# Differential attention on one core: the steps of TensorE written as two interleaved streams, one per row group

## What is computed

```python
Q = einsum('bse,hec->bhsc', X, Wq) + bq      # c = 2 * 64
K = einsum('bse,hec->bhsc', X, Wk) + bk
V = einsum('bse,hed->bhsd', X, Wv) + bv
A1 = einsum('bhqd,bhkd->bhqk', Q1, K1) * s   # first 64 of c
A2 = einsum('bhqd,bhkd->bhqk', Q2, K2) * s   # last 64 of c
P = softmax(A1) - lam * softmax(A2)
O = einsum('bhqk,bhkd->bhqd', P, V)
Y = concat_heads(O) @ Wo + bo                # then layer norm, gamma, beta
```

## Time and profile before

| | us |
|---|---|
| median of 3 runs | 1207.48 (1206.95 to 1208.09) |
| profiled execution | 1207.97 |
| its span, first to last instruction | 1206.2 |
| mean granted TensorE clock | 0.99 of 2.4 GHz |
| PE / POOL / ACT / DVE busy | 97% / 84% / 80% / 75% |

### The profile page before, as it was taken

How to read it: one execution, slowest core, us unless ns; L and a number is a source line. 1 busy time by engine, 2 the same in 40 slices (tenths; PEclk the granted TensorE clock), 3 DMA queues, 4 the chain that set the end, 5 groups by cost and what they waited for, 6 DMA issues and landing times.

```text
span 1206.2 us, 28081 instructions
## 1 busy us (share of the span) xinstructions
PE 1168.2 (97%) x9730; PEld 841.2 (70%) x9730; DVE 905.6 (75%) x1573; ACT 968.9 (80%) x1711; POOL 1017.3 (84%) x657
## 2 busy tenths in 40 slices
PE   5899999999999999999999999999999999998998
PEld 4666767666677776767676767676767776765797
DVE  8878878786787878887878887877887877874510
ACT  3398888887888888988888988888888888985432
POOL 3599999999999999999999999999999999989000
PEclk8999999999999999999999999999999999997999
DMA  8832211221112111222221112221112221110000
GB/s 208 312 80 51 50 44 49 49 49 42 23 39 49 49 49 44 49 49 49 49 49 40 30 34 49 49 49 43 49 49 49 49 49 42 25 28 1 1 18 18
DMA packets 74134, 63.41 MB, mean 53 GB/s; under 512 B 45172, under 2 KB 63092, under 8 KB 74100
## 3 DMA queue, kind: packets, MB, share of 16 engines
q1 hardware_dynamic: 73092, 62.78, 20.3%
q10 hardware_dynamic: 880, 0.19, 0.1%
q0 software_dynamic: 128, 0.01, 0.0%
HBM read 19.96 MB, written 9.44 MB: 24 GB/s over the span
## 4 chain that ended last, share of the span: by engine, by line
PE 75%; POOL 19%; DVE 4%; issue 1%; ACT 0%; DMA 0%; DVEq 0%; SPq 0%; POOLq 0%; ACTq 0%
PE ps L517 24%; PE ps L533 18%; PE ps L547 16%; POOL p_mix L431 11%; PE ps L472 7%; POOL work L428 5%; PE ps L559 4%; PE ps L611 3%; PE ps L598 2%; PE ps L499 1%; DVE pt L862 1%; DVE small L906 1%; POOL wqk_lo L343 1%; POOL w L406 0%; POOL wqk_hi L340 0%
## 5 line engine op out<-in xcount | busy, mean ns | idle before, releaser
L906 DVE TENSOR_REDUCE small<-ps 128x1 f32<-128x1024 f32 x512 | 613.8, 1220 | 114.6 <-PE ps L517 113.9
L431 POOL TENSOR_TENSOR p_mix<-p_mix,work 128x1024 f32<-128x1024 f32 x256 | 609.0, 2379 | 21.4
L533 PEld LDWEIGHTS ps<-ident,p_mix 64*128 64x128 f32 x4096 | 309.6, 139 | 191.7 <-issue 168.1
L725 ACT ACTIVATE pt<-ps 128x512 f32<-128x512 f32 x512 | 305.6, 597 | 131.2 <-PE ps L533 120.7
L533 PE MATMUL ps<-ident,p_mix 64*128 64x64 f32 x4096 | 352.6, 226 | 15.7 <-POOL p_mix L431 11.2
L428 POOL TENSOR_SCALAR work<-work,small 128x1024 f32<-128x1024 f32 x256 | 307.1, 1200 | 42.8 <-DVE small L931 42.8
L712 ACT ACTIVATE p_mix<-ps,small 128x1024 f32<-128x1024 f32 x256 | 284.8, 1113 | 15.4 <-DVE small L906 15.3
L712 ACT ACTIVATE work<-ps,small 128x1024 f32<-128x1024 f32 x256 | 284.4, 1111 | 12.5 <-DVE small L906 12.5
L547 PE MATMUL ps<-pt,v_h 128*64 128x512 f32 x1024 | 248.7, 606 | 0.0
L517 PE MATMUL ps<-k_hi,q_hi 64*128 64x512 f32 x512 | 234.4, 458 | 3.7 <-ACT p_mix L712 1.7
L517 PE MATMUL ps<-k_hi,qx_hi 64*128 64x512 f32 x512 | 230.5, 450 | 0.0
(11 more groups left out here) (135 smaller groups left out, 1305.3 us busy)
## 6 DMA issues: line engine op xcount, KB each, us to landing
qx_hi<-q_hi SPq DMA_DIRECT2D x64, 256.0 KB, 3.7
qx_lo<-q_lo SPq DMA_DIRECT2D x64, 256.0 KB, 4.6
v_scratch<-pt SPq DMA_DIRECT2D x16, 512.0 KB, 3.5
v_h<-v_scratch SPq DMA_DIRECT2D x32, 256.0 KB, 2.9
wqk_raw<-in_L_attn_Wk SPq DMA_DIRECT2D x31, 64.0 KB, 1.7
wqk_raw<-in_L_attn_Wq SPq DMA_DIRECT2D x31, 64.0 KB, 1.9
wo_dup<-in_L_attn_Wo SPq DMA_DIRECT2D x2, 512.0 KB, 7.1
w_raw<-in_L_ffn_W1e SPq DMA_DIRECT2D x4, 256.0 KB, 3.2
```

The lines of the kernel that those rows point to most:

```text
L431: pool.tensor_tensor(e1, e1, e2, ALU.add).then_inc(mix_done, 1)
L533: mm = pe.transpose(pt_ps[:, c * D:(c + 1) * D], p_mix[rows, col:col + P], ident[rows, rows])
L725: act.activation(pt4[:, kb % 2, :, j * P + half * D:j * P + (half + 1) * D], pt_ps.rearrange("p (c q) -> p c q", c=KC), ACT.Copy).then_inc ...
L906: dve.tensor_reduce(neg_max[:, m:m + 1], slot[SLOT[k, s]], AX.X, ALU.max, negate=True)\
```

## The change

PE's step is written anew. The twelve products become single calls (`product(g, k, s, t, half)`), and the transposes come in two calls of four (`turn(k, half, c0)`). T1 of step k moves from the end of step k to the start of step k + 1: its first four transposes stand behind the first product of tile (k + 1, 0), the second four behind the second. T0 of step k stands now among the last products of tile (k, 1), four behind `product(g, k, 1, 0, 0)` and four behind `product(g, k, 1, 1, 0)`. The products in between alternate row groups and take the last half of tile (k, 0) beside the first of tile (k, 1). So the wait for the slot of (k, 1) now stands ahead of the last products of (k, 0), and the waits of T0 (for the mix and for the copy of T1) ahead of the last two products of (k, 1). j == 2 is no longer an exception.

On DVE, `add_y` moves from the end of the step j == 1 to the start of the step j == 3, ahead of `inv_sums` and of the first maximum; `inv_sums` stands between the two maxima at j == 1 (before: j == 2) and after both at j == 0 and j == 2. DVE's tail is 8 steps long instead of 7. ACT, POOL and SP are as they were.

```diff
--- before.py
+++ after.py
@@ -503,23 +503,23 @@
 
             pe.wait_ge(v_evac, 2 * NT)
 
-            def scores(g, k, s):
-                tile = (k, s)
-                free = slot_free(g, tile)
+            def open_scores(g, k, s):
+                free = slot_free(g, (k, s))
                 if free:
                     pe.wait_ge(*free)
+
+            def product(g, k, s, t, half):
+
+
+                a, ax, b = ((q_hi, qx_hi, k_hi), (q_lo, qx_lo, k_hi), (q_hi, qx_hi, k_lo))[t]
                 q0, k0 = k // TB * S + (k % TB) * P, k // TB * S
-                for t, (a, ax, b) in enumerate(((q_hi, qx_hi, k_hi), (q_lo, qx_lo, k_hi), (q_hi, qx_hi, k_lo))):
-                    for half in range(2):
-
-                        r = (s + half) % 2
-                        rows = slice(r * D, (r + 1) * D)
-                        mm = pe.matmul(slot[SLOT[tile]][:, half * BANK:(half + 1) * BANK],
-                                       (ax if half else a)[rows, q0:q0 + P],
-                                       b[rows, k0 + half * BANK:k0 + (half + 1) * BANK], start=t == 0, stop=t == 2)
-                mm.then_inc(s_ready, 1)
-
-            def turn(g, k, half):
+                r = (s + half) % 2
+                rows = slice(r * D, (r + 1) * D)
+                return pe.matmul(slot[SLOT[k, s]][:, half * BANK:(half + 1) * BANK],
+                                 (ax if half else a)[rows, q0:q0 + P],
+                                 b[rows, k0 + half * BANK:k0 + (half + 1) * BANK], start=t == 0, stop=t == 2)
+
+            def open_turn(g, k, half):
 
                 n = g * BODY + k - LAG
                 if half == 0:
@@ -527,11 +527,14 @@
                 after(pe, pt_evac, 2 * n + half)
                 pe.nop(nofuse=True)
 
+            def turn(k, half, c0):
+
+
                 rows = slice(half * D, (half + 1) * D)
-                for c in range(KC):
+                for c in range(c0, c0 + KC // 2):
                     col = (k - LAG) % 4 * S + c * P
                     mm = pe.transpose(pt_ps[:, c * D:(c + 1) * D], p_mix[rows, col:col + P], ident[rows, rows])
-                mm.then_inc(pt_ready, 1)
+                return mm
 
             def pv(g, kb, c0):
 
@@ -566,13 +569,36 @@
                     if k % TB == 0:
                         pe.wait_ge(lo_done, 2 * (g * 2 + k // TB) + 2)
                         pe.wait_ge(q_crossed, 64 * (g * 2 + k // TB + 1))
-                    scores(g, k, 0)
-                    if j != 2:
-                        scores(g, k, 1)
+                    open_scores(g, k, 0)
+                    product(g, k, 0, 0, 0)
+
+                if now(g, k, LAG + 1):
+                    open_turn(g, k - 1, 1)
+                    turn(k - 1, 1, 0)
+                if now(g, k):
+                    product(g, k, 0, 1, 0)
+                if now(g, k, LAG + 1):
+                    turn(k - 1, 1, KC // 2).then_inc(pt_ready, 1)
+                if now(g, k):
+                    product(g, k, 0, 2, 0)
+                    product(g, k, 0, 0, 1)
+                    open_scores(g, k, 1)
+                    product(g, k, 1, 0, 1)
+                    product(g, k, 0, 1, 1)
+                    product(g, k, 1, 1, 1)
+                    product(g, k, 0, 2, 1).then_inc(s_ready, 1)
+                    product(g, k, 1, 2, 1)
+                    product(g, k, 1, 0, 0)
+
                 if now(g, k, LAG):
-                    turn(g, k, 0)
-                if j == 2 and now(g, k):
-                    scores(g, k, 1)
+                    open_turn(g, k, 0)
+                    turn(k, 0, 0)
+                if now(g, k):
+                    product(g, k, 1, 1, 0)
+                if now(g, k, LAG):
+                    turn(k, 0, KC // 2).then_inc(pt_ready, 1)
+                if now(g, k):
+                    product(g, k, 1, 2, 0).then_inc(s_ready, 1)
                 back = 1 if j == 3 else 2
                 if j in (3, 0) and now(g, k - j, back * QB):
                     pv(g, kb - back, 0 if j == 3 else 4)
@@ -584,8 +610,6 @@
                     if free:
                         pe.wait_ge(*free)
                     proj(g * 2 + k // TB + 1, PROJ_AT.index(k % TB), slot[SLOT[k, "proj"]])
-                if now(g, k, LAG):
-                    turn(g, k, 1)
 
             def hidden_mm(u):
                 b, i = divmod(u, (1 + TOPK) * HC)
@@ -931,11 +955,13 @@
                     dve.tensor_scalar(l1_neg[:, e:e + 1], l_sum[:, l:l + 1], lam_neg, None, ALU.mult)\
                         .then_inc(recip_done, 1)
 
+                if j == 3 and now(g, k - j, 2 * QB):
+                    add_y(g, kb)
                 if j == 3 and now(g, k, 1):
                     inv_sums()
                 if now(g, k):
                     row_max(g, k, 0)
-                if j == 2 and now(g, k, 1):
+                if j == 1 and now(g, k, 1):
                     inv_sums()
                 p = k - 1
                 if p % TB in PROJ_AT and now(g, p, -TB):
@@ -943,13 +969,11 @@
                              slot[SLOT[p, "proj"]])
                 if now(g, k):
                     row_max(g, k, 1)
-                if j < 2 and now(g, k, 1):
+                if j in (0, 2) and now(g, k, 1):
                     inv_sums()
                 if j == 0 and now(g, k - j, 2 * QB):
                     dve.wait_ge(pv_done, g * (BODY // QB) + kb - 1)
                     dve.tensor_copy(o_t[:, (kb % 2) * BANK:(kb % 2 + 1) * BANK], o_ps).then_inc(o_evac, 1)
-                if j == 1 and now(g, k - j, 2 * QB):
-                    add_y(g, kb)
 
             def norm_y(part):
                 half = part % 2
@@ -1001,7 +1025,7 @@
                     part = y_acc[:, (2 * b + quad) * BANK:(2 * b + quad + 1) * BANK]
                     dve.tensor_tensor(part, part, bank, ALU.add).then_inc(f_out, 1)
 
-            attention(dve, step, QB + 3)
+            attention(dve, step, 2 * QB)
             for part in range(9):
                 norm_y(part)
             for part in range(3 * B + 1):
```

## The result

The kernel after takes 1199.68 us (median of 7 runs, 1198.1 to 1203.0) against 1207.48 us for the kernel before (7 runs): a ratio of 0.9925, with a 95% interval from 0.9905 to 0.9945. It is faster by 7.8 us; 26.5 were forecast. The time lies in the stated range, near its upper end, and in the band of the second rival.

The account below looks back on a forecast made before the run. PE's chain was taken as the bound, POOL next. Eight steps falling from 32.86 to 31.8 us over 777 us give 25, earlier blocks 1 to 2: 1207.97 - 26.5 - 0.5 = 1181 us, range 1169 to 1203.

Parts of the forecast that it names:

- the second rival: PE's overlap partly lost by ordered starts or weight loads, 0.07 to 0.15 a batch: 1194 to 1209 us; chance 0.19.
- waits for slots at (2, 1) and (3, 1): Score tiles at j == 2 and 3 wait for ACT's exponentials: slots wanted at 3.99 and 8.21, got at 4.12 and 8.52.
- the walk: Handoffs between engines priced in order through one four-step block of the new kernel: 15.8 us against 16.43.
- Two signs of being right: PE's share of the span falls to about 90 to 93%; ACT's idle time before its copies of transposes shrinks.
- the two estimates: Added per eight steps: 0.17 us for ACT's bias copy, 0.15 where the first mix after the weight split meets its transposes.
- the cost of transposes beside products: On PE, between nothing and one product of the other group, 0.23 us, a batch; taken as nothing.
- The projection's handoff at j == 2: The projection waits for ACT's exponential of 4.46 and starts 1.26 us later, at 5.72.
- A lower clock is no rival of its own: PE kept granted clock 1.00 while busy 2.82 of 4 us between 58 and 62 us, and would be busier.
- POOL saturated (1): POOL never idles if the handoffs are priced a tenth too long: 1169.5 to 1174 us; chance 0.17.
- Slower (3): Each transpose batch on PE held by one product, 0.23 us, 0.9 a block: 1230 us; chance 0.12.
- No change in the starts (4): Hardware already reorders PE's starts, and waits at (2,1) and (3,1) take the gain: about 1207 us; chance 0.04.
- The DVE moves, costed at nothing: add_y and inv_sums in new places on DVE are covered; uncovered, add_y would cost up to 1.12 us a block.

Follow-up runs that it names:

- e7: Kernel after with T1 back at the end of its step, T0 still among the products: 1220.8 us.
- e4: Kernel after with all eight transposes T0 and their wait behind the last product of (k, 1): 1194.4 us.
- e1: Kernel after with the wait for the slot of (k, 1) moved behind the last two products of (k, 0) in every step: 1187.3 us.
- e6: Kernel after with GpSimd's scaling of the second map over 512 of its 1024 columns: 1189.4 us.
- e11: e5 with GpSimd's scaling of the second map over 512 of 1024 columns: 1160.4 us.
- e3: Kernel after with VectorE's order (add_y, inv_sums, tail) as in the kernel before: 1209.8 us.
- e10: Kernel after with add_y alone back in VectorE's step j == 1: 1205.1 us.
- e2: Kernel after with the slot wait of (k, 1) moved behind (k, 0)'s last two products at j == 2 and j == 3 alone: 1189.9 us.
- e5: Kernel after with the slot wait of (k, 1) behind (k, 0)'s last product and T0 with its waits behind all products: 1179.6 us.
- e8: Kernel before with VectorE's new order alone (add_y, inv_sums, tail): 1206.4 us.
- e9: e5 with ACT's copy of the next head's bias moved from behind the second exponential of step k % 8 == 0 to behind the first: 1178.6 us.

## Why the prediction was right and wrong

**Right.** The chain: PE held the block, and POOL was next but not far below. That T1 and T0 would run beside products, T1 at its old 0.52, is in the rows, and e7 shows that it is worth 0.47 a block. That relief of PE turns into waits for slots at (2, 1) and (3, 1) is in the rows, and the walk priced them well: over the 32 blocks the first maximum comes 1.65 after the step's start at j == 2 (walk: 1.61) and 1.83 at j == 3 (walk: 1.79). POOL's wait fell. Two signs of being right did not come: PE's share stayed at 95%, and ACT's idle time before its copies of the transposes grew, from 131 to 150 us. The Trainium skill, "TensorE: Matmul & The Clock Gate", the section on what happens when a matmul is issued, has matmuls stay in program order; e4's T0 starts ahead of a product that stands before it (600.98, 601.21), so here too the trace disagrees. Starts in order are not what was missing.

**Wrong: the size.** The walk's block of 15.8, 15.9 with the two estimates, was measured as 16.20, and 0.3 us over 47 blocks is 14 of the 18.7 us missed. The step that failed is the cost of transposes beside products:
- "I take nothing", and in the walk "T0 ends at S + 1.51 + 0.59": as written, T0 is followed by out_proj at j == 1 and by pv at j == 0 after 0.70, and at j == 3 after 0.67. At j == 0 and j == 1 this is 0.22 of the 0.38 that a block is over the walk. I took the low end, nothing, from three transposes beside one product. That was right for T1, and for T0's own pace, but not for the products of row group 1 that stand among T0's transposes. Taking T0 out from between them gives 0.61 to 0.63 at these two steps (e4).
- The rest is small: 0.06 at j == 0, where T0 starts at S + 1.57 on average and not at S + 1.51, and 0.06 at j == 3. There the second product after the slot's wait comes 0.34 later and not 0.25 (602.04 to 602.38). The handoff behind low_part, 0.07 in the walk and from no row, is larger too: behind a projection of K the next step starts 1.63 to 1.67 after low_part, 1.48 counted. The walk's 1.25 from a maximum to its exponential stands in neither of the rows that it names, but holds (1.26, from 602.95 to 604.21, in the kernel before).
- The projection's handoff at j == 2 was short, 1.26 counted and 1.49 measured (exponential at 614.29, projection at 615.78), but the next step's start makes it up: j == 2 is 0.02 over the walk.

The slot's wait ahead of the last products of (k, 0) is the largest single thing to mend, 0.19 a block (e1), but it is no part of the miss, since the walk had it. I priced an order with a fault in it and did not see that the fault could be taken out.

**Wrong: the clock.** "A lower clock is no rival of its own", since PE would "be busier than that", was read from one stretch of 4 us. The clock did fall, once, in the first steps, and the start lost 2.3 us instead of gaining (how much of it by the clock is open, as said above). The tail lost about 2 as well: from the out_proj at 1075.19 before and 1064.95 after to the end of the span it is 131.0 and 132.9 us. That was not taken apart.

**The rivals.** POOL saturated (1): e6 and e11 refute it for the steady loop; it is true for the first 16 blocks. The overlap partly lost (2): its number came out, 1194 to 1209, and with it T0's half of its cause. T0's batches lag by 0.08 to 0.11, inside its 0.07 to 0.15; T1's do not, ordered starts are not the reason, and weight loads are what the rows point at (e4). It was given a chance of 0.19 and is nearest to what happened. Slower (3): not seen with the change whole; with its T1 part left out, e7 is slower by 1%. No change in the starts (4): refuted, a block is 0.23 shorter; but e4 shows that T0 needed no rewriting to run beside products. The DVE moves, costed at nothing, cost nothing where they are, but e3 shows that the change is worth 0.22 a block less without them, and the prediction did not say so.

## What to carry to other kernels

A wait in an in-order list holds all that stands behind it, so in two interleaved streams the place of a wait has to be chosen as carefully as the place of the work (here 0.19 us a block against 0.47 for T1's place): finish what is ready, then wait. When a walk of the new order shows such a wait, try the order without it before building. Where the hardware already looks past instructions of the other row group, interleave only what it can't reach (T1, ahead of a whole step's products) and leave the rest in plain order (T0). When one engine's step gets shorter, look again at orders of the others that were harmless: the sums between two maxima cost nothing before and 0.18 of the gain of 0.23 us a block after. And take the mean over many blocks before naming the cause of a miss: the single step read first here was one of the longer kind, and pointed at the wrong term.

## What the runs showed of the hardware

- TensorE starts matmuls of one row group ahead of older ones of the other: T0 at 600.98 before the product of 601.21 (e4). Three products in a row on row group 1 did not starve row group 0 (e1).
- Transposes of 64 x 128 on one row group keep their pace of 60 to 65 ns beside products of 512 columns on the other: T1's eight in 0.49 us in the kernel after. A product that stands among them in the program came 0.33 us after the one before it, and 0.23 when it stood ahead of them (e4).
- After a wait, the second product on a row group comes 0.34 us after the first, in a running stream 0.23.
- The granted clock fell to half for some 7 us between 50 and 70 us in both profiles of the kernel after, behind PE's longer waits of the first steps, and for some 3 to 14 us in e3, e4, e6 and e10 too; the kernel before, e1, e2, e5, e7, e8, e9 and e11 kept the upper level there.
